# Adjacency products with residual and layer norm: first x in two halves on SyncE's queue, later x on ScalarE's queue, a new order at both ends

## Chip, cores and metric

One core of a Trainium2 chip runs the whole program. The metric is the time of one execution on the device in microseconds (us); less is better.

## What is computed

For each of 8 batches there are x (1024 rows of 128 floats) and an adjacency matrix adj of 1024 x 1024 int32. With these inputs adj holds only 0 and 1, so of the four relations only the first has a mask that is not empty.

```python
masks = (relation[None] == rel_ids[:, None, None, None]).astype(x.dtype)
h = jnp.einsum('rbnm,bmd->rbnd', masks, x)
y = jnp.einsum('rbnd,rdo->bno', h, weight)
...
x = _layernorm(x + y + bias)
```

## The kernel before, in words

A batch is cut into 8 units of 128 rows of adj. The kernel is written engine by engine, each with its own program in a fixed order, and semaphores between them; nothing is scheduled by a planner. What the engines do for a batch b:

- SyncE issues the loads of adj in pairs of units (`load_adj`, 1 MB each, 8 KB in one piece for each partition; the ten units of the start are loaded alone with `load_unit`, 512 KB each in pieces of 4 KB) and of x (`load_x`, 512 KB). adj has three slots, so the load for batch b waits until batch b-3 has been transposed and checked in that place. x has a place of its own for every batch. All these loads, and after them all stores, go through SyncE's one DMA queue (q1 in the profile); only the first x and the bias go through ScalarE's queue (q10).
- `step(b)` says how rows lie on partitions: with step J (8) a partition holds eight neighbouring rows of x, which is one piece of 4 KB; with step 2 it holds two neighbours in four places, so x moves in pieces of 1 KB. For adj it decides the stride at which TensorE reads.
- TensorE transposes each unit (`transpose_unit`), VectorE copies the transposed unit out as a mask (`mask_unit`), TensorE multiplies x by it in two parts, `x_hi` and `x_lo`, for a group of units (`products`), ScalarE copies the result (`copy_h`), and TensorE multiplies that by the weights (`project`). Batches 2 to 6 are two groups of 4 units each. TensorE takes turns: a transposed unit of the next group, then a quarter of the products of this one.
- ScalarE makes `x_hi` (`split_hi`) and reads every pair of adj once more to test that it holds only 0 and 1 (`check`); GpSimd makes `x_lo` from `x_hi`, adds the bias, and normalises the rows; VectorE adds y and x (`sum_rows`) and takes the statistics.
- The last batch is cut finer: groups a (4 units), c (2), e (1) and d (1), with the rows of the last two batches shared out among ScalarE, GpSimd and VectorE, and a matmul with `found` that says whether a second pass for other inputs is needed (it is not entered with these inputs).

The products of a batch wait for the whole `x_hi` of that batch, and `x_hi` waits for the landing of the whole x. ScalarE's program for the groups is one loop: `copy_h` of the group before, in the last group of a batch `split_hi` of the next batch, then the checks, and behind the first of them `root`, the square root for the batch before.

Of the kernel before, what the change touches and what calls it, by code (L numbers as in the profile page):

```python
# [5 lines left out]
P = 128  # L6
FP32 = mybir.dt.float32
# [32 lines left out]
def adj_resnorm_kernel(nc, x, adj, weight, bias, out):  # L40
# [14 lines left out]
    def step(b):  # L55
        return J if b < EARLY else 2
# [61 lines left out]
    with ctx:  # L118
# [9 lines left out]
        ident = sb("ident", [P, P], BF16)  # L128
        ones = sb("ones", [P, 1], FP32)
# [55 lines left out]
        s_unit = [[sem(f"unit_loaded{b}{u}") if alone(b, u) else None for u in range(J)] for b in range(EARLY)]  # L185
        s_x = [sem(f"x_loaded{b}") for b in range(B)]
# [5 lines left out]
        s_ident = sem("ident_ready")  # L192
        s_const = sem("constants_ready")
# [197 lines left out]
        def _(sp):  # L391
            def load_x(b):
                sp.dma_start(units_of(x_sb[:, b], b, 0, J), rows_of(x, b, 0, J)).then_inc(s_x[b], 16)  # L393

# [15 lines left out]
            load_unit(0, 0)  # L410
            load_unit(0, 1)
# [4 lines left out]
            load_x(1)  # L416
# [21 lines left out]
        def _(pool):  # L438
# [3 lines left out]
                                    base=0, pattern=[[-1, P]], channel_multiplier=1).then_inc(s_ident, 1)  # L442

# [58 lines left out]
            normalise(full, full.units[:4])  # L502
# [6 lines left out]
        def _(act):  # L509
            def check(b, k):  # L510
# [15 lines left out]
            def split_hi(b, js, signal):  # L526
                act.wait_ge(s_x[b], 16)
# [24 lines left out]
            split_hi(0, slice(0, HALF), s_hi0)  # L552
            split_hi(0, slice(HALF, J), s_hi)
# [23 lines left out]
            normalise(full, full.units[4:5])  # L577
            copy_h(e)
            root(ra)
            normalise(full, full.units[5:7])  # L580
            copy_h(d)
            normalise(full, full.units[7:]).then_inc(s_aside, 1)
# [286 lines left out]
```

## Time and profile before

| what | value |
|---|---|
| median of 3 runs | 120.64 us (120.59 to 120.68) |
| the profiled execution, whole | 120.54 us |
| its span, first to last instruction | 118.8 us |
| TensorE busy | 106.6 us, 90% |
| ScalarE busy | 88.1 us, 74% |
| VectorE busy | 84.8 us, 71% |
| GpSimd busy | 70.3 us, 59% |
| DMA | 42.22 MB, 355 GB/s over the span |
| granted TensorE clock, mean | 0.985 |

The shares are means over the whole span. The profile further cuts the span in 40 slices, follows the chain of work that ended last, and lists what every engine waited for; times in those views count from the first instruction.

### The profile page before, as it was taken

To read this page: it belongs to the slowest core of one execution; us is meant where nothing else is said; L and a number is where in the kernel's file an instruction comes from. 1 tells how busy PE (TensorE), PEld (TensorE's weight loads), DVE (VectorE), ACT (ScalarE), POOL (GpSimd) and SP (SyncE) were. 2 spreads that over 40 slices of the span, in tenths; PEclk is the share of its full clock that TensorE was granted. 3 is DMA by queue.
4 is the path that set the end of the run, shared out by engine and by line. 5 is a ranking of instruction groups with operands and counts; after the bars stand their busy time and mean duration, and the time that the engine had idled before them with its cause. 6 is when DMAs were issued, how large, how long until landed. Compare 5 with 4: busy or idle time off the path is not lost.

```text
span 118.8 us, 2879 instructions
## 1 busy us (share of the span) xinstructions
PE 106.6 (90%) x1012; PEld 80.4 (68%) x1023; DVE 84.8 (71%) x252; ACT 88.1 (74%) x114; POOL 70.3 (59%) x132
## 2 busy tenths in 40 slices
PE   6788999899999979999999999999999999999400
PEld 2168898799997646767676767676868676679300
DVE  1055678397877848696959887787779777998840
ACT  4088277947797999799999499968987698925530
POOL 2007001940047998399569955995689577977740
PEclk9999999999999999999999999999999999999985
DMA  3999999999999999999999999999999999450271
GB/s 73 389 408 411 414 407 422 414 391 412 425 414 384 419 403 436 380 414 414 419 391 404 422 406 394 420 406 423 377 433 411 415 399 383 141 177 0 85 248 35
DMA packets 12419, 42.22 MB, mean 355 GB/s; under 512 B 882, under 2 KB 7155, under 8 KB 8947
## 3 DMA queue, kind: packets, MB, share of 16 engines
q1 hardware_dynamic: 12256, 41.49, 88.6%
q10 hardware_dynamic: 146, 0.52, 1.3%
q8 instruction: 9, 0.15, 0.5%
q14 instruction: 8, 0.06, 0.1%
HBM read 37.81 MB, written 4.19 MB: 354 GB/s over the span
## 4 chain that ended last, share of the span: by engine, by line
PE 58%; DMA 29%; SPq 5%; DVE 2%; issue 1%; ACT 0%; DVEq 0%
PE h_ps L619 32%; DMA adj_sb<-adj 29%; PE ids_t L601 16%; PE y_ps L633 9%; SPq L396 4%; PE ids_t L633 1%; DVE x_sb L758 0%; SPq L393 0%; SPq L412 0%; ACT std L539 0%; DVE stats L711 0%; DVE x_sb L705 0%; DVE moments L717 0%; DVEq L255 0%; DVE shift L751 0%
## 5 line engine op out<-in xcount | busy, mean ns | idle before, releaser
L522 ACT ACTIVATE junk<-adj_sb,minus 128x2048 bf16<-128x2048 int32 x32 | 63.8, 1994 | 0.4 <-DMA adj_sb<-adj 0.4
L699 DVE TENSOR_SCALAR mask_t<-ids_t 128x1024 bf16<-128x1024 uint16 x64 | 43.6, 687 | 25.2 <-PE ids_t L601 24.1
L601 PEld LDWEIGHTS ids_t<-ident,adj_sb 128*128 128x128 bf16 x512 | 36.5, 123 | 13.8 <-DMA adj_sb<-adj 2.7
L601 PE MATMUL ids_t<-ident,adj_sb 128*128 128x128 bf16 x512 | 40.0, 221 | 2.3 <-DMA adj_sb<-adj 2.2
L619 PE MATMUL h_ps<-mask_t,x_lo 128*128 128x512 bf16 (+2 forms) x184 | 33.5, 314 | 0.0
L619 PE MATMUL h_ps<-mask_t,x_hi 128*128 128x512 bf16 (+2 forms) x173 | 31.1, 310 | 1.2 <-DVE mask_t L699 0.6
L448 POOL TENSOR_TENSOR x_lo<-x_sb,x_hi 128x1024 f16<-128x1024 f32 x7 | 15.0, 2144 | 24.2 <-ACT x_hi L531 24.2
L488 POOL TENSOR_SCALAR x_sb<-x_sb,rstd,shift 128x128 f32<-128x128 f32 x55 | 24.0, 457 | 1.0
L535 ACT ACTIVATE h_all<-h_ps 128x512 f32<-128x512 f32 (+2 forms) x23 | 10.6, 463 | 18.1 <-PE h_ps L619 18.1
L454 POOL TENSOR_TENSOR x_sb<-x_sb,bias_sb 128x1024 f32<-128x1024 f32 x8 | 19.0, 2377 | 7.8 <-DVE x_lo L764 7.7
L619 PEld LDWEIGHTS h_ps<-mask_t,x_hi 128*128 128x128 f16 x184 | 15.6, 98 | 7.2 <-DVE mask_t L699 1.2
L619 PEld LDWEIGHTS h_ps<-mask_t,x_lo 128*128 128x128 f16 x184 | 16.4, 98 | 5.9
L633 PE MATMUL y_ps<-w_sb,h_all 128*128 128x128 f32 x120 | 17.8, 284 | 0.0
L633 PEld LDWEIGHTS y_ps<-w_sb,h_all 128*128 128x128 f32 x120 | 15.0, 192 | 0.1
L711 DVE BATCH_NORM_STATS2 stats<-x_sb 128x6 f32<-128x128 f32 x64 | 14.5, 280 | 0.1
L705 DVE TENSOR_TENSOR x_sb<-y_ps,x_sb 128x512 f32<-128x512 f32 (+2 forms) x20 | 11.0, 552 | 1.9 <-PE y_ps L633 1.0
L531 ACT ACTIVATE x_hi<-x_sb 128x1024 f16<-128x1024 f32 (+1 forms) x9 | 8.5, 954 | 3.1 <-DMA x_sb<-x 3.1
L692 DVE TENSOR_REDUCE row_max<-x_hi 128x8 f32<-128x1024 f16 x8 | 9.6, 1202 | 0.0
L522 ACT ACTIVATION_READ_ACCUMULATOR junk<-adj_sb,minus 128x1 f32 x32 | 6.1, 190 | 0.0
L640 PE MATMUL h_ps<-mask_t 128*128 128x512 bf16 x11 | 4.6, 586 | 1.2 <-DVE mask_t L787 1.2
L717 DVE BATCH_NORM_AGGREGATE moments<-stats 128x2 f32<-128x6 f32 x64 | 5.3, 154 | 0.1
L470 POOL TENSOR_TENSOR product<-sixteenth,first_guess 128x8 f32<-128x8 f32 (+1 forms) x8 | 1.6, 203 | 6.2 <-DVE first_guess L727 6.0
(44 smaller groups left out, 30.8 us busy)
## 6 DMA issues: line engine op xcount, KB each, us to landing
adj_sb<-adj SPq DMA_DIRECT2D x27, 1024.0 KB, 19.5
adj_sb<-adj SPq DMA_DIRECT2D x10, 512.0 KB, 8.4
x_sb<-x SPq DMA_DIRECT2D x7, 512.0 KB, 18.9
out<-x_sb SPq DMA_DIRECT2D x7, 512.0 KB, 16.7
x_sb<-x ACTq DMA_DIRECT2D x1, 512.0 KB, 5.4
out<-x_sb SPq DMA_DIRECT2D x2, 256.0 KB, 3.3
w_sb<-weight SPq DMA_DIRECT2D x1, 64.0 KB, 6.1
bias_row<-bias ACTq DMA_DIRECT2D x1, 0.5 KB
```

The source lines that it names most:

```text
L448: nc.gpsimd.tensor_tensor(x_lo[:, b % 2], x_sb[:, b], x_hi[:, b % 2], ALU.subtract).then_inc(s_lo, 1)
L454: nc.gpsimd.tensor_tensor(x_sb[:, b], x_sb[:, b], bias_sb[:, :].unsqueeze(1).to_broadcast([P, J, D]), ALU.add).then_inc(s_xb, 1)
L488: last = nc.gpsimd.tensor_scalar(rows[:, slot, u, :], rows[:, slot, u, :], rstd[:, slot, u:u + 1], shift[:, slot, u:u + 1], ALU.mult, ALU.add)
L522: nc.scalar.activation(junk[:, at % 2], adj_sb[:, slot, 2 * k:2 * k + 2, :], ACT.Square, scale=2.0, bias=minus[:, 0:1], accum_out=squares[ ...
L535: nc.scalar.activation(h_all[:, g.bank, 0:g.count * P], h_ps[g.bank][:, 0:g.count * P], ACT.Copy).then_inc(s_h, 1)
L601: last = nc.tensor.transpose(bank[:, j, :], words[:, j // step(b), j % step(b), 0, :], ident[:, :])
L619: last = nc.tensor.matmul(h_ps[g.bank][:, 0:g.count * P], part[:, g.b % 2, j, :], mask_t[:, g.b % 2, j, g.cols], start=(j == 0 and part is ...
L633: last = nc.tensor.matmul(y_of(g)[:, n, :], h_all[:, g.bank, n * P:(n + 1) * P], w_sb[:, 0, :], start=True, stop=True)
L692: nc.vector.tensor_reduce(row_max[:, b, :], x_hi[:, b % 2], AX.X, ALU.max, apply_absolute_value=True).then_inc(s_rm, 1)
L699: nc.vector.tensor_scalar(mask_t[:, b % 2, :, u * P:(u + 1) * P], ids_t[u % T_BANKS][:, :, :].bitcast(UINT16), 1.0, None, ALU.mult).then_i ...
L705: nc.vector.tensor_tensor(rows[:, g.b, g.us, :], y_of(g)[:, 0:g.count, :], x_sb[:, g.b, g.us, :], ALU.add).then_inc(s_sum, 1)
L711: last = nc.vector.bn_stats(stats[:, u, :], rows[:, g.b, u, :])
```

## The change

There are four parts.

1. The first x no longer comes by ScalarE's queue. It comes as two halves on SyncE's queue, behind the first unit of adj and ahead of the second, with a semaphore for each half.
2. x of the batches 1 to 7 leaves SyncE's queue. ScalarE issues it on its own queue: in the first group of batch b (in the second for batch 0) the x of batch b+1. `split_hi` moves behind the first check of its group and behind `root`. Batch 1 now has step 2 instead of J.
3. At the start TensorE makes one idle matmul less, and transposes the units 2 and 3 of the first batch a step earlier.
4. At the end TensorE adds the x of the last unit with a matmul by an fp32 identity (`add_x`; GpSimd makes that identity at the start), so VectorE takes statistics of group d from PSUM without `sum_rows`; the matmul with `found` comes behind that; of batch 6's rows ScalarE normalises six instead of four, GpSimd two instead of four.

```diff
     def step(b):
-        return J if b < EARLY else 2
+        return J if b == 0 else 2
...
             load_unit(0, 0)
+            for n in range(2):
+                sp.dma_start(x_sb[:, 0, n * HALF:(n + 1) * HALF, :], rows_of(x, 0, n * HALF, HALF)).then_inc(s_x0[n], 16)
             load_unit(0, 1)
...
             load_unit(1, 0)
-            load_x(1)
             load_unit(1, 1)
             for k in range(1, PAIRS):
                 load_adj(1, k)
-            load_x(2)
-            for b in range(EARLY, B):
+            for b in range(2, B):
                 for k in range(PAIRS):
                     load_adj(b, k)
-                if b + 1 < B:
-                    load_x(b + 1)
...
-            normalise(full, full.units[:4])
+            normalise(full, full.units[:2])
...
+            def load_x(b):
+                act.dma_start(units_of(x_sb[:, b], b, 0, J), rows_of(x, b, 0, J)).then_inc(s_x[b], 16)
...
-            act.dma_start(units_of(x_sb[:, 0], 0, 0, J), rows_of(x, 0, 0, J)).then_inc(s_x[0], 16)
...
                 copy_h(groups[g.index - 1])
-                if ends_batch(g):
-                    split_hi(b + 1, slice(0, J), s_hi)
+                if b + 1 < B and g.place == (0 if b else 1):
+                    load_x(b + 1)
                 todo = range(pairs_checked_by(groups[g.index - 1]), pairs_checked_by(g))
                 for n, at in enumerate(todo):
                     check(at // PAIRS, at % PAIRS)
-                    q = groups[g.index - 2] if g.index >= 2 else None
-                    if n == 0 and q and ends_batch(q):
-                        root(sets[q.b])
+                    if n == 0:
+                        q = groups[g.index - 2] if g.index >= 2 else None
+                        if q and ends_batch(q):
+                            root(sets[q.b])
+                        if ends_batch(g):
+                            split_hi(b + 1, slice(0, J), s_x[b + 1], s_hi)
...
+            def add_x(g):
+
+                pe.wait_ge(s_whole, 1)
+                pe.wait_ge(s_xb, g.b + 1)
+                nc.tensor.matmul(y_of(g)[:, 0, :], whole_ident[:, :], x_sb[:, g.b, g.first, :], start=True, stop=False)
...
             project(e)
+            add_x(d)
+            project(d)
             pe.wait_ge(s_found, 1)
             nc.tensor.matmul(ids_t[0][0:1, 0, 0:2].bitcast(FP32), found[:, :], ones[:, :],
                              start=True, stop=True).then_inc(s_count, 1)
-            project(d)
...
-            for g in (e, d):
-                sum_rows(g)
-                statistics(g)
+            sum_rows(e)
+            statistics(e)
+            statistics_of_sum(d)
```

Three places show how the rows move. On ScalarE, over one batch in the middle (batch 4: the second `x_hi` row is the x of batch 5), the order before is this; L522 is a check, L535 `copy_h`, L531 `split_hi`, L539 `root`.

```order
L535 ACTIVATE h_all<-h_ps 128x512
L522 ACTIVATE junk,squares<-adj_sb,minus 128x2048 x2
L535 ACTIVATE h_all<-h_ps 128x512
L531 ACTIVATE x_hi<-x_sb 128x1024
L522 ACTIVATE junk,squares<-adj_sb,minus 128x2048
L539 ACTIVATE std<-moments,eps 128x8
L522 ACTIVATE junk,squares<-adj_sb,minus 128x2048
```

The same batch in the changed kernel, where L526 is a check, L539 `copy_h`, L535 `split_hi`, L543 `root` and L512 the new load:

```order
L539 ACTIVATE h_all<-h_ps 128x512
L512 DMA x_sb<-x 128x4x256
L526 ACTIVATE junk,squares<-adj_sb,minus 128x2048 x2
L539 ACTIVATE h_all<-h_ps 128x512
L526 ACTIVATE junk,squares<-adj_sb,minus 128x2048
L543 ACTIVATE std<-moments,eps 128x8
L535 ACTIVATE x_hi<-x_sb 128x1024
L526 ACTIVATE junk,squares<-adj_sb,minus 128x2048
```

The load of x stands behind the first `copy_h` of the batch, and `x_hi` one check and `root` later than before; between load and use stand two checks, a `copy_h`, a third check and `root`.

On SyncE, from the start of the program, the rows that go and come (with their - and +) are these; L393 and L412 of the new file are the block's head and the halves of x.

```order
-L396 DMA adj_sb<-adj 128x1024 x2
-L412 DMA w_sb<-weight 128x128
-L396 DMA adj_sb<-adj 128x1024 x7
-L393 DMA x_sb<-x 128x1024
+L412 DMA x_sb<-x 128x512 x2
+L396 DMA adj_sb<-adj 128x1024
+L414 DMA w_sb<-weight 128x128
+L396 DMA adj_sb<-adj 128x1024 x8
+L403 DMA adj_sb<-adj 128x2048 x27
```

Behind the start, SyncE's queue now holds the 27 pairs of adj in one run, with no x between them, and then the stores.

On TensorE, the end before (L619 `products`, L633 `project`, L678 the matmul with `found`):

```order
L619 MATMUL h_ps<-mask_t,x_lo 128x128 x8
L633 MATMUL ids_t<-w_sb,h_all 128x128
L678 MATMUL ids_t<-ones,found 1x1
L633 MATMUL ids_t<-w_sb,h_all 128x128
L255 TENSOR_LOAD again
```

and now, with L647 as `add_x`:

```order
L639 MATMUL ids_t<-w_sb,h_all 128x128
L647 MATMUL ids_t<-x_sb,whole_ident 128x128
L639 MATMUL ids_t<-w_sb,h_all 128x128
L692 MATMUL ids_t<-ones,found 1x1
L258 TENSOR_LOAD again
```

The identity matmul stands between the last two projections, and the matmul with `found` behind both.

## Rows read from the trace of the kernel before

**Rows 1.** Page: span, ScalarE's busy time, and DMA in 40 slices (busy tenths).

```profile
span 118.8 us, 2879 instructions
...
PE 106.6 (90%) x1012; PEld 80.4 (68%) x1023; DVE 84.8 (71%) x252; ACT 88.1 (74%) x114; POOL 70.3 (59%) x132
...
DMA  3999999999999999999999999999999999450271
```

**Rows 2.** Chain that ended last: start us, us, what; its first line gives shares.

```profile
PE 58%; DMA 29%; SPq 5%; DVE 2%; issue 1%; ACT 0%; DVEq 0%
...
24.82 18.44 DMA adj_sb<-adj
...
50.18 0.81 PE h_ps L619 x3
...
62.56 0.81 PE h_ps L619 x3
...
74.93 0.81 PE h_ps L619 x3
...
87.30 0.81 PE h_ps L619 x3
...
99.68 0.81 PE h_ps L619 x3
```

**Rows 3.** Timeline of TensorE around 43 us: start us, us, what, idle before.

```profile
43.30 0.64 PE L601 MATMUL ids_t<-ident,adj_sb 128*128 128x128 bf16 x8 [0.58 <-DMA adj_sb<-adj]
```

**Rows 4.** DMA issues: KB each, median us from issue to landing.

```profile
adj_sb<-adj SPq DMA_DIRECT2D x27, 1024.0 KB, 19.5
...
x_sb<-x SPq DMA_DIRECT2D x7, 512.0 KB, 18.9
...
x_sb<-x ACTq DMA_DIRECT2D x1, 512.0 KB, 5.4
```

**Rows 5.** DMA queues in 2.5 to 4.5 us: packets, MB, share of 16 engines.

```profile
q1 hardware_dynamic: 77, 0.32, 46.6%
q10 hardware_dynamic: 77, 0.32, 38.6%
```

**Rows 6.** DMA packets and q1 in 56 to 60 us.

```profile
DMA packets 252, 1.68 MB, mean 420 GB/s; under 512 B 26, under 2 KB 50, under 8 KB 50
...
q1 hardware_dynamic: 252, 1.68, 101.5%
```

**Rows 7.** DMA packets and q1 in 61 to 63 us, while an x passes.

```profile
DMA packets 341, 0.82 MB, mean 410 GB/s; under 512 B 16, under 2 KB 273, under 8 KB 273
...
q1 hardware_dynamic: 341, 0.82, 109.5%
```

**Rows 8.** Instructions of lines 393 and 403: ns min/median/max, first and last start us.

```profile
L393 SPq DMA_DIRECT2D x_sb<-x x7: 429/1862/3792, 6.3 to 67.8; - x7
...
L403 SPq DMA_DIRECT2D adj_sb<-adj x27: 385/2102/6860, 7.2 to 77.8; - x27
```

**Rows 9.** Timeline of ScalarE: start us, us, what.

```profile
36.89 0.39 ACT L535 ACTIVATE h_all<-h_ps 128x256 f32<-128x256 f32 x1 [0.72 <-PE h_ps L619]
...
49.72 0.60 ACT L535 ACTIVATE h_all<-h_ps 128x512 f32<-128x512 f32 x1 [0.86 <-PE h_ps L619]
50.22 2.00 ACT L522 ACTIVATE junk<-adj_sb,minus 128x2048 bf16<-128x2048 int32 x1
...
52.20 2.00 ACT L522 ACTIVATE junk<-adj_sb,minus 128x2048 bf16<-128x2048 int32 x1
...
56.66 1.05 ACT L531 ACTIVATE x_hi<-x_sb 128x1024 f16<-128x1024 f32 x1
57.61 1.99 ACT L522 ACTIVATE junk<-adj_sb,minus 128x2048 bf16<-128x2048 int32 x1
```

**Rows 10.** ScalarE's groups in 49.7 to 99 us: busy us, mean ns, idle before.

```profile
L535 ACT ACTIVATE h_all<-h_ps 128x512 f32<-128x512 f32 x8 | 4.8, 595 | 6.9 <-PE h_ps L619 6.9
```

**Rows 11.** Timeline of the end: two rows on ScalarE, TensorE's last projection, VectorE's sum and statistics.

```profile
109.50 0.86 ACT L545 ACTIVATE x_sb<-x_sb,shift,rstd 128x128 f32<-128x128 f32 x2
...
110.74 0.49 PE L633 MATMUL ids_t<-w_sb,h_all 128*128 128x128 f32 x2
...
111.26 0.29 DVE L705 TENSOR_TENSOR x_sb<-ids_t,x_sb 128x128 f32<-128x128 f32 x1
...
111.59 0.29 DVE L711 BATCH_NORM_STATS2 stats<-x_sb 128x6 f32<-128x128 f32 x1
```

**Rows 12.** GB/s in 40 slices of 110 to 118.8 us (0.22 us each).

```profile
GB/s 0 0 0 0 0 0 0 37 0 158 340 321 344 340 372 349 145 51 0 0 261 358 303 289 326 400 354 56 14 9 23 33 19 23 23 5 0 0 0 0
```

More of the change, by code:

```diff
@@ L185, in adj_resnorm_kernel @@
         s_unit = [[sem(f"unit_loaded{b}{u}") if alone(b, u) else None for u in range(J)] for b in range(EARLY)]
+        s_x0 = [sem(f"half_of_first_x_loaded{n}") for n in range(2)]
         s_x = [sem(f"x_loaded{b}") for b in range(B)]
@@ L192, in adj_resnorm_kernel @@
         s_ident = sem("ident_ready")
+        s_whole = sem("whole_ident_ready")
         s_const = sem("constants_ready")
@@ L442, in _ @@
                                     base=0, pattern=[[-1, P]], channel_multiplier=1).then_inc(s_ident, 1)
+            pool.wait_ge(s_ident, 1)
+            nc.gpsimd.tensor_copy(whole_ident[:, :], ident[:, :]).then_inc(s_whole, 1)
             def split_lo(b):
@@ L524, in check, with split_hi @@
                                      accum_out=squares[:, at:at + 1]).then_inc(s_check, 1)
-            def split_hi(b, js, signal):
-                act.wait_ge(s_x[b], 16)
+            def split_hi(b, js, loaded, signal):
+                act.wait_ge(loaded, 16)
                 if b >= 2:
@@ L547, in normalise @@
                 return last
-            act.dma_start(units_of(x_sb[:, 0], 0, 0, J), rows_of(x, 0, 0, J)).then_inc(s_x[0], 16)
             act.dma_start(bias_row[:, :], bias.rearrange("(a d) -> a d", a=1)).then_inc(s_bias, 16)
             act.preload_act_table(ACT.Sqrt)
-            split_hi(0, slice(0, HALF), s_hi0)
-            split_hi(0, slice(HALF, J), s_hi)
+            split_hi(0, slice(0, HALF), s_x0[0], s_hi0)
+            split_hi(0, slice(HALF, J), s_x0[1], s_hi)
             act.wait_ge(s_spread, 1)
@@ L576, in _ @@
             copy_h(c)
-            normalise(full, full.units[4:5])
+            normalise(full, full.units[2:3])
             copy_h(e)
             root(ra)
-            normalise(full, full.units[5:7])
+            normalise(full, full.units[3:5])
             copy_h(d)
-            normalise(full, full.units[7:]).then_inc(s_aside, 1)
+            normalise(full, full.units[5:]).then_inc(s_aside, 1)
             root(rb)
@@ L633, in project @@
                     last = nc.tensor.matmul(y_of(g)[:, n, :], h_all[:, g.bank, n * P:(n + 1) * P], w_sb[:, 0, :],
-                                            start=True, stop=True)
+                                            start=g.index < len(groups) - 1, stop=True)
                 last.then_inc(s_y, 1)
+            def add_x(g):
+                pe.wait_ge(s_whole, 1)
+                pe.wait_ge(s_xb, g.b + 1)
+                nc.tensor.matmul(y_of(g)[:, 0, :], whole_ident[:, :], x_sb[:, g.b, g.first, :], start=True, stop=False)
             def idle_turns(n):
@@ L642, in _ @@
             pe.wait_ge(s_still, 1)
-            idle_turns(9)
+            idle_turns(8)
             pe.wait_ge(s_ident, 1)
@@ L654, in _ @@
             products(g, 1, 2)
+            transpose_unit(0, 2)
             g = groups[1]
             products(g, 0, 2)
-            transpose_unit(0, 2)
+            transpose_unit(0, 3)
             project(groups[0])
             products(g, 1, 2)
-            transpose_unit(0, 3)
             for g in groups[2:LAST + 1]:
@@ L712, in statistics, with statistics_of_sum @@
                 last.then_inc(s_st, 1)
+            def statistics_of_sum(g):
+                dve.wait_ge(s_y, g.index + 1)
+                nc.vector.bn_stats(stats[:, g.first, :], y_of(g)[:, 0, :]).then_inc(s_st, 1)
             def combine(r, g, units):
@@ L752, in shift_rows, with normalise @@
                                                in1=rstd[:, r.b, r.us], op0=ALU.mult, op1=ALU.mult).then_inc(s_rstd_last, 1)
-            def normalise(r, units):
+            def normalise(r, u, source):
                 wait_for_rstd(dve, r)
-                slot = r.b
-                for u in units:
-                    last = nc.vector.tensor_scalar(rows[:, slot, u, :], rows[:, slot, u, :], mean[:, slot, u:u + 1],
-                                                   rstd[:, slot, u:u + 1], ALU.subtract, ALU.mult)
-                last.then_inc(s_done, 1)
+                return nc.vector.tensor_scalar(rows[:, r.b, u, :], source, mean[:, r.b, u:u + 1], rstd[:, r.b, u:u + 1],
+                                               ALU.subtract, ALU.mult)
             def split_lo(b, js, hi, lo):
@@ L849, in _ @@
                 part(rb)
-            normalise(rb, rb.units[2:])
+            normalise(rb, e.first, rows[:, rb.b, e.first, :])
+            normalise(rb, d.first, y_of(d)[:, 0, :]).then_inc(s_done, 1)
             second_pass(dve, second_dve)
```

3 lines of the change are left out of this document (1 added, 2 removed).

## The prediction

> **What bounds the kernel now.** I read the page first: DMA stands at 9 tenths in every slice from the second to the 34th, and TensorE is busy 90% of the span [rows 1]. So two resources are nearly full at once, and the chain must say which one ends last where. It gives TensorE 58% and DMA 29% [rows 2]. Its last DMA piece runs from 24.82 us for 18.44 us; there TensorE waits 0.58 us for the first pair of batch 3 [rows 3]. Up to 43.3 us the arrival of bytes sets the pace. From there no DMA stands in the chain, only TensorE: the products of the batches 3 to 7 begin at 50.18, 62.56, 74.93, 87.30 and 99.68 [rows 2] (the units of each are transposed one group ahead). A batch takes 12.37 us, and its products begin only when its whole `x_hi` is there. That is the deadline the change touches.
>
> x meets it now with ease: it rides in SyncE's queue, 18.9 us from issue to landing, but issued far ahead [rows 4, 8]; ScalarE makes the `x_hi` of batch 4 at 56.66, some 5 us ahead of 62.56 [rows 9].
>
> **Part 2, the later x.** Bytes do not change, only their queue. What matters is how the 16 DMA engines share themselves between two queues that are both full. The one place where the trace shows it is the start, when the first x (q10) meets the units of adj (q1), both in pieces of 4 KB: in 2.5 to 4.5 us each queue moved 77 packets [rows 5]. One for one. That fits a turn for each piece, and it fits equally a turn for each so many bytes, since the pieces were of one size. Now they are not: x comes in pieces of 1 KB, and what it meets are pairs of adj in pieces of 8 KB. One for one in pieces gives x one ninth of the bytes.
>
> The durations: in 56 to 60 us q1 moved 252 packets at a share of 1.015 of 16 engines, that is 65 us of engine time; 50 of them were small, about 2 us, so an 8 KB piece takes 63/202 = 0.31 us [rows 6]. In 61 to 63 us, with 341 packets of which 68 were large (21.3 us of 35.0), the 257 pieces of 1 KB took 0.053 us each [rows 7]. x is 512 pieces, 32 for each engine, so its transfer is 32 x (0.31 + 0.053) = 11.6 us. Each adj load gives an engine 8 pieces and one small completion write, which I count as a turn as well: some 3.6 of the 32 turns cost nothing, 1.1 us less, 10.5 us. Around that lies the fixed part: the first x landed after 5.4 us [rows 4] while its 4 KB pieces, 8 for each engine, at an even share of about 0.16 us each would take 2.6 us and the cold start more; I take 1.5 us of the rest. Landing time L = 12.0 us. The bounds are 5.4 us from the nearest row, if 1 KB pieces are served by bytes, and 13 us with all turns paid.
>
> What ScalarE does in that time [rows 9]: `copy_h` 0.50 us from start to start, a check 1.98, `x_hi` 0.95, `root` 0.2. Issue costs 0.43 us, the least that SyncE shows for an x [rows 8]. After the issue come two checks (4.4 us with the issue), then `copy_h`, which waits for TensorE until about 6.2 us after the issue, a check and `root`: ScalarE comes to `split_hi` 8.9 us after the issue. With L = 12.0 it waits 3.1 us. Behind that wait stand a check, `copy_h` of the batch's last group, and then the issue of the next x. So the issues form a ring that TensorE does not set: L + 0.95 + 1.98 + 0.50, with a few hundredths for semaphores L + 3.45 = 15.45 us, against 12.37 us of TensorE. The ring decides from L = 8.9 us on.
>
> Now step by step. The issue of batch 3's x comes behind the `copy_h` at 36.89, at 37.3 us [rows 9]. `x_hi` is ready at issue + L + 1.05.
> - Batch 3: 37.3 + 13.05 = 50.35, needed at 50.18: 0.2 us late.
> - Batch 4: issued 52.75, ready 65.8, needed 62.56: 3.2 late.
> - Batch 5: issued 68.2, ready 81.25, needed 74.93: 6.3 late.
> - Batch 6: issued 83.65, ready 96.7, needed 87.30: 9.4 late.
> - Batch 7: issued at 99.1. The last pair of adj is issued at 77.8 and needs 19.5 us [rows 4, 8], so q1 has run out at 97 us; this x lands in some 4 us, ScalarE's own 8.9 us decide again, and `x_hi` is ready at 109.1, just when TensorE has done batch 6 (99.68 + 9.4). No further loss.
>
> That adj keeps q1 full until then in spite of the late TensorE is an assumption: the last loads, for batch 7, wait until ScalarE has checked batch 4, which it does with the two checks behind the issue at 68.2, by 73 us; the last of them is issued at 77.8 us now. It holds with 5 us to spare.
>
> Batches 1 and 2: x 1 meets adj pieces of 4 KB (0.16 us each, half of 0.31) and lands after 1.5 + 32 x 0.21 = 8.3 us, under the 8.9; x 2 lands after 12 us, and its batch has three checks behind the issue (L522 x3 in the first group), which brings ScalarE to `split_hi` 2 us later than 8.9. I cost both at 0; if that cover is gone, TensorE's wait for adj at 43.30 [rows 3] takes up the first 0.58 us of it.
>
> `x_hi` one check later, 2.2 us: covered by the 5 us above. If x comes in time this costs nothing, for GpSimd's `x_lo` is needed only in the second half of the products. ScalarE's idle time, 6.9 us in four batches or 1.7 for each [rows 10], covers the issue.
>
> **Part 1 and 3, the start.** The first unit of adj no longer shares its way with x, so the first transposes start sooner. But the second unit has the same bytes ahead of it as before, and by 43.3 us the pace is that of bytes: the gain is used up there. 0; the bounds are 0.6 us less, if x 3 is still under way when the first pair of batch 3 lands and so lets it pass (TensorE waited 0.58 us for it), and 0.2 us more, for x 1 in 1 KB pieces instead of 4 KB (512 x 0.053 against 128 x 0.16 us over 16 engines, 0.4 us at most).
>
> **Part 4, the end.** Without `sum_rows` of d, VectorE takes statistics at about 111.35 instead of 111.59 [rows 11]: the last projection at 110.74 now starts behind the identity matmul. That is 0.2 us less on the chain. But ScalarE has two rows more of batch 6 in front of its store, 0.86 us by the two it does at 109.50 [rows 11], and the three last stores move closer together. The stores run at 300 to 370 GB/s with a pause of 0.6 us between them [rows 12]; a later first store fills that pause. I take 0 for the end, between 0.2 less and 0.3 more.
>
> **Sum.** 120.54 for the profiled execution + 9.4 + 0 + 0 = 129.9 us; the median of the runs lies 0.1 above it, so 130.0. In L it goes as 4L - 38.5: 5.5 us at L = 11, and beyond 12.5 it stops growing near 11, since x 6 then finds q1 empty.
>
> **Rivals.**
> - *Bytes, not pieces* (not slower). If the engines share by bytes, or take 4 KB of a queue at a time, x needs 8 x (0.31 + 0.21) = 4.2 us and lands after 5.7: ahead of ScalarE's 8.9. For it: equal packets in rows 5 were equal bytes too. Against it: nothing in these rows packs small pieces together; each 1 KB is a packet of its own in the profile's count [rows 7]. The time is 120.5, from 119.9 (x 3 lets adj pass, and 0.2 at the end) to 120.9.
> - *A whole load in one turn* (not slower). An engine would finish all 9 pieces of an adj load, 2.6 us, and then all of x, 1.7 us; x lands within 6 us, and the time is again 120.5. Against it: in rows 5 both queues moved evenly, where x, which started first, should have been done before q1 moved. The Trainium skill, DMA: Bandwidth & Descriptors, Queues, rings and completion order, says that an engine goes round its queues by whole packets, typically of 9 to 17 descriptors; by that the change would cost nothing, and the even counts do not look like it.
> - *The issue blocks ScalarE* (slower, by another cause). SyncE's issues of x take 1.86 us in the middle and up to 3.79 where its queue is full [rows 8]. If ScalarE's issue is held up behind SyncE's, 1.7 us of idle time [rows 10] cover the median. At 3.8 us the other 2.1 go into each of four batches: 8 us, 129. For it: nothing; the ScalarE queue holds one x only. It decides from about 2.1 us.
>
> **Chances.** Pieces, slow x: 0.60, with 126 to 132.5 as its own range. Bytes or whole loads: 0.35, of which faster 0.22 and the same 0.13. Blocked issue: 0.05. A change of less than 0.2% (0.24 us) can't be told from none here. Slower 0.65, same 0.13, faster 0.22. The likeliest is 130.0; the range must take in the second case, 120.0, and ends at 132.5.
>
> **What would show it.** In the profile after, x on ScalarE's queue lands 11 to 13 us after its issue; ScalarE waits for x at `x_hi` in the batches 4 to 6, about 3 us each; TensorE waits for `x_hi` at the first products of the batches 4, 5 and 6, and its issues lie 15 to 16 us apart. In the short windows behind an issue, packets of q10 and q1 are even in number and one to eight in bytes. I am wrong if x lands in 6 us or so: then ScalarE never waits for x, and the time stays near 120.5. If instead the issue on ScalarE takes 2 us and more, it is the third rival.

## The result

The changed kernel takes 137.26 us (median of 4 runs, 135.47 to 139.75) against 120.66 for the kernel before on the same chip: the ratio is 1.130, with an interval of 1.120 to 1.140. Two of the four runs (137.65 and 139.75) fell in a slower state of the chip, and the ratios, here and below, compare only runs outside it. The forecast was 130.0 us, with 120.0 to 132.5 as its range. The direction and the kind of wait were right, and the time lies outside the range.

The page of the profiled execution (136.88 us, span 135.1) in the lines that answer to [rows 1]. PEclk is the granted clock in tenths; the group lines give busy time and mean length, and behind the second bar the idle time before them and what ended it.

```profile
span 135.1 us, 2882 instructions
...
PE   6769988999937999289996999259999999999700
...
PEclk9999999999996899968999999977999999999975
DMA  4999999999999999999999999999961340004063
...
q1 hardware_dynamic: 9616, 38.34, 71.9%
q10 hardware_dynamic: 3698, 3.67, 7.9%
...
PE 45%; DMA 19%; issue 10%; SPq 7%; POOL 7%; DVE 5%; ACT 2%; DVEq 0%; ACTq 0%
...
L535 ACT ACTIVATE x_hi<-x_sb 128x1024 f16<-128x1024 f32 (+1 forms) x9 | 8.6, 958 | 21.1 <-DMA x_sb<-x 21.0
...
x_sb<-x ACTq DMA_DIRECT2D x7, 512.0 KB, 15.0
```

TensorE's row shows four dips that were not there before, and ScalarE waits 21.0 us in all for x at `x_hi`: 17.6 of them for the x of the batches 2 to 5, the rest for the first x, for which the kernel before waited 3.1 us as well. One x needs 15.0 us from issue to landing as a median. The DMA engines move the same bytes as before and stay full to the 29th slice; what is late is one load among them, not the bytes as a whole.

ScalarE's timeline shows the wait and what stands behind it (start, length, engine, line, operation, idle time before it; ACTq is the queue on which ScalarE issues):

```profile
40.03 1.06 ACT L535 ACTIVATE x_hi<-x_sb 128x1024 f16<-128x1024 f32 x1 [4.09 <-DMA x_sb<-x]
40.04 0.38 ACTq L512 DMA_DIRECT2D x_sb<-x  x1
40.99 0.36 ACT L539 ACTIVATE h_all<-h_ps 128x256 f32<-128x256 f32 x1
41.26 1.99 ACT L526 ACTIVATE junk<-adj_sb,minus 128x2048 bf16<-128x2048 int32 x1
...
48.35 0.60 ACT L539 ACTIVATE h_all<-h_ps 128x512 f32<-128x512 f32 x1 [1.03 <-PE h_ps L625]
48.84 2.00 ACT L526 ACTIVATE junk<-adj_sb,minus 128x2048 bf16<-128x2048 int32 x1
...
56.47 1.06 ACT L535 ACTIVATE x_hi<-x_sb 128x1024 f16<-128x1024 f32 x1 [4.79 <-DMA x_sb<-x]
56.62 0.37 ACTq L512 DMA_DIRECT2D x_sb<-x  x1
```

The x of batch 3 is issued at 40.04 and its `x_hi` starts at 56.47, 16.4 us later. Then the issue of the next x follows within 0.15 us, although `copy_h` (L539) of the group before stands ahead of it in the program: the issue goes out as soon as the wait in front of it is over, not when the queued activations have run. So the loads form a ring, wait for x, issue of the next x, wait for that one, and it is as long as one landing: the issues of x 3 to 6 lie at 40.04, 56.62, 71.80 and 87.96.

TensorE pays. These are the first products of the batches 2, 3, 4 and 5, with TensorE's idle time before them:

```profile
41.40 0.98 PE L625 MATMUL h_ps<-mask_t,x_hi 128*128 128x512 bf16 x2 [2.86 <-issue]
...
57.84 0.59 PE L625 MATMUL h_ps<-mask_t,x_hi 128*128 128x512 bf16 x2 [2.90 <-issue]
...
73.03 0.59 PE L625 MATMUL h_ps<-mask_t,x_hi 128*128 128x512 bf16 x2 [1.21 <-DVE mask_t L712]
...
89.19 0.98 PE L625 MATMUL h_ps<-mask_t,x_hi 128*128 128x512 bf16 x2 [3.85 <-issue]
```

The profile names another releaser or none, but each of the four begins 0.31 or 0.32 us behind the end of its `x_hi` (for batch 3, 56.47 + 1.06 = 57.53, and 57.84): it is `x_hi` that they wait for. The batches 3, 4 and 5 begin at 57.84, 73.03 and 89.19 where [rows 2] had 50.18, 62.56 and 74.93: 7.7, 10.5 and 14.3 us late. Batch 2 begins at 41.40, where the trace of before has 37.48: 3.9 us late. Batches 6 and 7 begin at 103.23 and 115.61 in this trace, both 15.9 us late. The last projection begins at 127.37, where [rows 11] had 110.74: 0.7 more, of which 0.3 comes back behind it, so that the span is 16.3 us longer.

The step from batch 5 to batch 6 holds no wait for x: x 6 was there (its `x_hi` ran at 99.88, ahead of 103.23). It took 14.04 us against 12.37 before, and the windows of this kernel say why. Their columns are the stretch, its length, then for each engine busy time and instructions, the granted clock, the DMA share and GB/s:

```profile
72.00:75.00 3.00, 1.98 (x16) 1.30 (x18) 3.00 (x7) 3.00 (x4) 2.14 (x1) 1.00 1.03 426
75.00:88.00 13.00, 10.29 (x96) 7.42 (x95) 8.38 (x27) 7.12 (x10) 7.29 (x16) 1.00 1.02 408
88.00:91.00 3.00, 1.81 (x9) 1.12 (x11) 1.22 (x1) 3.00 (x4) 2.05 (x1) 0.71 1.00 410
91.00:103.00 12.00, 11.95 (x104) 8.25 (x103) 7.56 (x22) 10.22 (x13) 9.37 (x18) 0.93 0.79 294
```

After the idle time of 3.85 us the granted clock was 0.71 in 88 to 91 us, so part of it at the lower level, 1.2 GHz. The first half of batch 5 then took 7.86 us (89.19 to 97.05), the second, at full clock, 6.18 (97.05 to 103.23): 1.7 us. The clock fell in the same way behind the idle times of 2.86 and 2.90 us (0.68 in 40 to 44 and 0.69 in 57 to 61), and not behind 1.21 us (1.00 in 72 to 75). It costs time only once: in the batches 2 to 4 x came later than TensorE at either clock.

### The profile page after: what moved, and what is told of

Read it like the earlier page. It is cut to its first block, busy times and chain, and to the rows that moved or that the text cites. A ratio compares the mean times of both kernels' runs of the same rounds, so it can differ in the third digit from the quotient of the medians.

```text
span 135.1 us, 2882 instructions
## 1 busy us (share of the span) xinstructions
PE 111.4 (82%) x1013; PEld 82.5 (61%) x1024; DVE 86.3 (64%) x251; ACT 89.1 (66%) x116; POOL 69.6 (52%) x131
## 4 chain that ended last, share of the span: by engine, by line
PE 45%; DMA 19%; issue 10%; SPq 7%; POOL 7%; DVE 5%; ACT 2%; DVEq 0%; ACTq 0%
PE h_ps L625 25%; DMA adj_sb<-adj 19%; PE ids_t L607 14%; PE y_ps L639 6%; SPq L396 4%; SPq L403 3%; POOL x_sb L488 3%; DVE mask_t L712 2%; POOL x_sb L454 2%; ACT x_sb L549 1%; ACT x_hi L535 1%; DVE moments L735 1%; DVE stats L724 1%; SPq L412 1%; POOL x_lo L448 1%
## 5 line engine op out<-in xcount | busy, mean ns | idle before, releaser
L526 ACT ACTIVATE junk<-adj_sb,minus 128x2048 bf16<-128x2048 int32 x32 | 63.8, 1993 | 1.6 <-DMA adj_sb<-adj 1.5
L607 PEld LDWEIGHTS ids_t<-ident,adj_sb 128*128 128x128 bf16 x512 | 37.4, 121 | 16.9 <-DMA adj_sb<-adj 4.6
L607 PE MATMUL ids_t<-ident,adj_sb 128*128 128x128 bf16 x512 | 41.6, 226 | 3.4 <-DMA adj_sb<-adj 3.3
L625 PE MATMUL h_ps<-mask_t,x_hi 128*128 128x512 bf16 (+2 forms) x173 | 34.8, 333 | 11.5 <-issue 9.6
L625 PEld LDWEIGHTS h_ps<-mask_t,x_hi 128*128 128x128 f16 x184 | 16.2, 101 | 18.6 <-issue 11.5
L488 POOL TENSOR_SCALAR x_sb<-x_sb,rstd,shift 128x128 f32<-128x128 f32 x53 | 23.0, 449 | 1.3 <-DVE shift L769 0.4
L535 ACT ACTIVATE x_hi<-x_sb 128x1024 f16<-128x1024 f32 (+1 forms) x9 | 8.6, 958 | 21.1 <-DMA x_sb<-x 21.0
L625 PEld LDWEIGHTS h_ps<-mask_t,x_lo 128*128 128x128 f16 x184 | 16.5, 99 | 6.0
L539 ACT ACTIVATE h_all<-h_ps 128x512 f32<-128x512 f32 (+2 forms) x23 | 10.5, 455 | 13.5 <-PE h_ps L625 13.5
L526 ACT ACTIVATION_READ_ACCUMULATOR junk<-adj_sb,minus 128x1 f32 x32 | 6.0, 188 | 0.0
L549 ACT ACTIVATE x_sb<-x_sb,shift,rstd 128x128 f32<-128x128 f32 x9 | 4.0, 486 | 1.4 <-POOL shift L481 1.1
L652 PE MATMUL h_ps<-mask_t 128*128 128x512 bf16 x10 | 3.8, 539 | 1.2 <-DVE mask_t L802 1.2
```

Source lines behind the costliest of these rows:

```text
L488: last = nc.gpsimd.tensor_scalar(rows[:, slot, u, :], rows[:, slot, u, :], rstd[:, slot, u:u + 1], shift[:, slot, u:u + 1], ALU.mult, ALU.add)
L526: nc.scalar.activation(junk[:, at % 2], adj_sb[:, slot, 2 * k:2 * k + 2, :], ACT.Square, scale=2.0, bias=minus[:, 0:1], accum_out=squares[ ...
L535: nc.scalar.activation(x_hi[:, b % 2, js], x_sb[:, b, js], ACT.Copy).then_inc(signal, 1)
L539: nc.scalar.activation(h_all[:, g.bank, 0:g.count * P], h_ps[g.bank][:, 0:g.count * P], ACT.Copy).then_inc(s_h, 1)
L607: last = nc.tensor.transpose(bank[:, j, :], words[:, j // step(b), j % step(b), 0, :], ident[:, :])
L625: last = nc.tensor.matmul(h_ps[g.bank][:, 0:g.count * P], part[:, g.b % 2, j, :], mask_t[:, g.b % 2, j, g.cols], start=(j == 0 and part is ...
```

## How the two queues share the DMA engines

In 44 to 50 us, with both queues full (columns: packets, MB, share of 16 engines):

```profile
q1 hardware_dynamic: 288, 2.11, 86.2%
q10 hardware_dynamic: 290, 0.30, 14.4%
```

288 and 290: as many pieces of the one queue as of the other, 2.11 MB to 0.30. That is the sharing that the prediction worked with; of its rivals, shares by bytes fell here. The transfer ran from 43.67 to 55.64, 12 us, and the rival of whole loads in one turn fell with it.

Even counts over 6 us would also come out if each queue had turns of nine pieces, and so would a time near 12 us: the 32 pieces of x on an engine would then pass in four turns, each behind an adj load's eight pieces of 0.31 us (an estimate: 4 x 2.5 + 32 x 0.053 = 11.7 us). The first 0.36 us of the transfer (43.64 to 44) tell the two apart:

```profile
q1 hardware_dynamic: 18, 0.13, 88.4%
q10 hardware_dynamic: 17, 0.02, 13.8%
```

The first 17 pieces of x, about one for each of the 16 engines, all start before 43.94, and none starts from there to 44.03. There the second round begins, 0.32 us behind the end of the first piece of x, and a piece of adj takes 0.31 to 0.32. So one piece passes in a turn. The Trainium skill, DMA: Bandwidth & Descriptors, Queues, rings and completion order, has an engine take a whole packet, typically of 9 to 17 descriptors, from one queue before it switches. The measurement decides against it.

What the prediction had not seen is the time ahead of the first piece. The same view for 40.04 to 43.64, from the issue of x 3 until its first piece, has no row for q10 at all:

```profile
DMA packets 212, 1.52 MB, mean 421 GB/s; under 512 B 27, under 2 KB 27, under 8 KB 27
q1 hardware_dynamic: 212, 1.52, 101.5%
issues: line engine op xcount, KB each, median us to landing
adj_sb<-adj SPq DMA_DIRECT2D x1, 1024.0 KB, 21.7
x_sb<-x ACTq DMA_DIRECT2D x1, 512.0 KB, 16.4
```

3.6 us pass, in which SyncE's queue moves 1.52 MB, although every other turn should belong to x. It is the same for each x from 1 to 6: 3.5 to 3.7 us. With SyncE's queue empty (x 7, issued at 102.78) the first piece moves after 1.0 us, and x lands 3.6 us after its issue. So the landing of x 3 is 3.6 us to the first piece, 12 us of transfer and about 0.8 to the semaphore: 16.4. For x 2 to 5 it is 15.0 to 16.5 us, with transfers of 10.6 to 12.3.

## The experiments

### The queue alone, and everything but the queue

`queue_alone` is the kernel before with one part of the change: x 1 to 7 on ScalarE's queue, one batch ahead.

```diff
# ScalarE
                 copy_h(groups[g.index - 1])
+                if b + 1 < B and g.place == (0 if b else 1):
+                    load_x(b + 1)
                 if ends_batch(g):
                     split_hi(b + 1, slice(0, J), s_hi)
# SyncE: load_x(1), load_x(2) and load_x(b + 1) taken out
```

> The kernel before with only the loads of x 1 to 7 moved to ScalarE's queue, one batch ahead; x_hi stays ahead of the check, both ends stay as before. Theory (the queue costs everything): x lands 15 to 16.5 us after its issue and the time is 133 to 140 us. Rival (the other parts share the blame): under 130 us.

137.54 us, ratio 1.136 (1.129 to 1.144). Its ScalarE rows read like those of the changed kernel; the three x waited for are those of the batches 2 to 4:

```profile
39.22 1.06 ACT L527 ACTIVATE x_hi<-x_sb 128x1024 f16<-128x1024 f32 x1 [5.66 <-DMA x_sb<-x]
39.37 0.38 ACTq L504 DMA_DIRECT2D x_sb<-x  x1
...
55.61 1.06 ACT L527 ACTIVATE x_hi<-x_sb 128x1024 f16<-128x1024 f32 x1 [6.62 <-DMA x_sb<-x]
56.21 0.37 ACTq L504 DMA_DIRECT2D x_sb<-x  x1
...
72.51 1.06 ACT L527 ACTIVATE x_hi<-x_sb 128x1024 f16<-128x1024 f32 x1 [4.76 <-DMA x_sb<-x]
```

`x_on_sync` is the changed kernel with the loads of x 1 to 7 back in their old places on SyncE.

> The changed kernel with only the loads of x 1 to 7 put back into SyncE's queue, in their old places. Theory (the queue costs everything): TensorE waits for x_hi nowhere after batch 2, and the time is 120.2 to 121.0 us. Rival (a good part of the 16 us comes from the later place of x_hi, the step of batch 1, or the two ends): above 122 us, with TensorE waiting for x_hi or x_lo although x has landed long before.

122.37 us, ratio 1.011 (1.010 to 1.013), and no wait for a later x is left. So the queue alone makes the whole loss, behind which the other parts don't show; by themselves those cost 1.4 us together, which prediction and expectation had at nothing; they are taken apart below.

### Is it lateness, or the queue as such?

`two_ahead` leaves x on ScalarE's queue and issues it one batch sooner.

```diff
-                if b + 1 < B and g.place == (0 if b else 1):
-                    load_x(b + 1)
+                if b == 0 and g.place in (1, 3):
+                    load_x(1 if g.place == 1 else 2)
+                if b and b + 2 < B and g.place == 0:
+                    load_x(b + 2)
```

> The changed kernel with x of batch b+2 instead of b+1 issued in the first group of batch b (x 1 and x 2 both in batch 0). Theory (x is late by its slow share alone, nothing else of the queue costs): x still needs 15 to 16.5 us, but has some 21, so ScalarE waits for no x and the time is 120.0 to 121.5 us. Rival (traffic on two queues slows adj, or the issue on ScalarE costs): above 123 us.

122.69 us, ratio 1.016 (1.014 to 1.017). x still lands after 16.0 us as a median, and the waits for it are down to 0.2 us in all. That shows the mechanism: what costs is that one batch is shorter than a landing. The number lies 1.8 us above the kernel before and so outside the expectation; 1.4 of it are the other parts', which `x_on_sync` had shown as well.

### The length of the pieces

`adj_4k` loads the pairs of adj from batch 2 on unit by unit, so that x meets pieces of 4 KB; `x_4k` gives x pieces of 4 KB (step J in every batch) and leaves adj at 8 KB.

```diff
# adj_4k
+                for u in (2 * k, 2 * k + 1):
+                    sp.dma_start(adj_sb[:, slot, u:u + 1, :], rows_of(adj, b, u, 1)).then_inc(s_adj[slot][k], 16)
# x_4k
     def step(b):
-        return J if b == 0 else 2
+        return J
```

> The changed kernel with each pair of adj from batch 2 on loaded by two DMAs in pieces of 4 KB instead of one in pieces of 8 KB; x and its place as in the changed kernel. Theory (one piece of x for each piece of adj): the 32 pieces of an engine take 32 x 0.21 = 6.8 us instead of 11.9. If the 3.6 us ahead of the first piece are a number of adj pieces, they halve too, and x lands in 9.5 us, time 120.5 to 122.5; if they are a fixed time, x lands in 11.3 us, time 121 to 126. Rival (x has a fixed share of the bytes, whatever the pieces): x lands after 15 to 16 us as now, time 134 to 139.

> The changed kernel with step J for every batch, so x moves in pieces of 4 KB (128 instead of 512) and adj in 8 KB as now; TensorE reads adj at a wider stride, 0.07 us more for each unit of batches 1 to 7. Theory (one piece for one piece): x takes 8 x 0.47 = 3.8 us behind the first 3.6 and lands about 8.3 us after its issue; no wait for x, and the time is 123 to 126 us by the stride. Rival (an x on this queue is slow by a share of bytes): x lands in 15 us or more, time above 134.

`adj_4k`: 125.37 us, ratio 1.037 (1.035 to 1.039). `x_4k`: 122.47 us, ratio 1.012 (1.010 to 1.014), no wait for a later x, and a little less than expected. In `adj_4k` `x_hi` still waits for x, 8.7 us in six waits, and the last line gives the landing of the ACTq loads (least, median, greatest):

```profile
  ACT x_hi L539: 8.7, 6
...
DMA to landing us min/median/max: 11.3/11.8/12.2
```

The landings in `x_4k`:

```profile
DMA to landing us min/median/max: 6.9/8.6/9.3
```

The transfer follows the turns. With adj pieces of half the length it took 7.5 us (54.95 to 62.42) in place of 12; with a quarter as many pieces of x 4.7 us (54.67 to 59.38). The time ahead of the first piece did not follow: 3.6 and 3.5 us (51.38 to 54.95, and 51.19 to 54.67), with 1.43 and 1.39 MB of SyncE's queue ahead. It is not a number of adj's pieces (some 180 of 8 KB, some 350 of 4 KB), nor of x's.

### Where do the 3.6 us come from?

`three_in_flight` and `two_in_flight` let SyncE issue a pair of adj only when the pair three, or two, before it has landed.

```diff
             def load_adj(b, k):
                 slot = b % ADJ_SLOTS
+                if b >= 2:
+                    c, m = divmod(PAIRS * b + k - 3, PAIRS)   # - 2 in two_in_flight
+                    sp.wait_ge(s_adj[c % ADJ_SLOTS][m], loads_of(c, m))
```

> The changed kernel, where SyncE issues a pair of adj (from batch 2 on) only when the pair three before it has landed, so its queue holds at most 3 MB and never blocks. It tells apart what the 3.6 us between the issue of x and its first piece are. Theory A (ScalarE's descriptors wait behind SyncE's blocked issue): the first piece moves about 1 us after the issue, x lands in 13 to 14 us, and the time falls to 124 to 131 us. Theory B (each engine has a stock of adj pieces taken in already, some ten, whatever SyncE does): 3.3 to 3.8 us stay, x lands in 15 to 16.5 us, time 133 to 139.

> As the run with three pairs of adj in flight, but two. There the first piece of x moved 1.9 to 3.6 us after its issue, in the changed kernel 3.6, with an idle SyncE queue 1.05. Theory A (the delay is waiting behind what SyncE has issued and the queue has not taken in): 1 to 2 us, x lands in 12.5 to 14 us, time 123 to 131 us. Theory B (a time that any full engine adds): 3 us and more remain, time 131 us or above.

`three_in_flight`: 133.14 us, ratio 1.099 (1.096 to 1.103). The time lies in theory B's range, but neither theory held for the delay: the times to the first piece scatter, 2.7, 3.0, 1.9, 3.6 and 2.5 us for x 2 to 6. The shortest, from the issue at 54.85 to 56.7, had 0.72 MB ahead:

```profile
q1 hardware_dynamic: 93, 0.72, 97.9%
```

`two_in_flight`: 126.42 us as the mean of the two runs behind its ratio of 1.046 (1.043 to 1.050), 128.66 as the median of all five; its trace is of a run of 130.52. The times to the first piece go down to 1.0 us for two of the loads and are 2.2 to 3.6 for the others. No x from 1 to 7 is waited for there; TensorE now waits for adj, by up to 1.28 us at a time, since SyncE issues too late to keep the engines full. So the time ahead depends on what SyncE's queue has issued. Limiting it makes the changed kernel faster, but not as fast as the kernel before.

`adj_1k` and `adj_512b` change the rate: from batch 2 on each pair of adj comes as four loads of 256 columns, or eight of 128.

```diff
+                cuts = 1 if b < 2 else 4                      # 8 in adj_512b
+                for n in range(cuts):
+                    cols = slice(n * N // cuts, (n + 1) * N // cuts)
+                    sp.dma_start(units_of(adj_sb[:, slot], b, 2 * k, 2)[..., cols],
+                                 rows_of(adj, b, 2 * k, 2)[..., cols]).then_inc(s_adj[slot][k], 16)
```

> The changed kernel with every load of adj from batch 2 on cut into four loads of 256 columns each, so that adj moves in pieces of 1 KB like x. Bytes theory (SyncE's queue has a fixed 1.4 to 1.5 MB ahead of a newly issued x, as it had at 8 KB and at 4 KB): pieces of 1 KB took 0.053 us each on 16 engines, about 310 GB/s, so x's first piece moves 4.6 to 4.8 us after the issue. Time theory (a fixed delay of the second queue while the first is full): 3.5 us again. Either way x then has half of all pieces and half of the bytes, 512 x 2 x 0.053 / 16 = 3.4 us of transfer.

> The same with eight loads of 128 columns, pieces of 512 bytes. The rate of such pieces isn't known from a run here and is read from this one. Bytes theory: the delay to x's first piece is 1.45 MB divided by that rate, above 5 us if the rate is below 290 GB/s. Time theory: 3.5 us. A third theory, that loads count and not bytes, would give fewer bytes ahead than 1.4 MB in both of these kernels, since each load is now a quarter or an eighth of a pair.

One run each: 129.71 and 176.16 us, beside 120.57 for the kernel before. For `adj_1k` the packets from an x issue at 54.07 to its first piece:

```profile
DMA packets 1338, 1.31 MB, mean 347 GB/s; under 512 B 79, under 2 KB 1336, under 8 KB 1336
q1 hardware_dynamic: 1336, 1.29, 106.6%
```

3.8 us and 1.29 MB. By loads, a pair and a half would have been 0.4 MB: that theory fell. A fixed time (3.5 to 3.6) misses by 5 to 9%, a fixed stock (1.39 to 1.52 MB, at 347 GB/s 4.0 to 4.4 us) by 5 to 15%, so these two are not told apart. In `adj_512b` the small pieces came at 192 to 198 GB/s, SyncE's loads landed 2.9 us after their issue, and q1 held 70 to 72% of the engines; there the first piece of x moved 1.1 us after its issue (63.27 to 64.3), about as with an empty queue. The delay belongs to engines that are full with a backlog behind them. What holds that backlog is not shown.

### The 1.4 us beside the queue

Three kernels go back from `x_on_sync` part by part, and one puts a single part into the kernel before.

```diff
# first_x_back = x_on_sync and, for the two halves on SyncE:
+            act.dma_start(units_of(x_sb[:, 0], 0, 0, J), rows_of(x, 0, 0, J)).then_inc(s_x[0], 16)
# first_x_and_step_back = that and
-        return J if b == 0 else 2
+        return J if b < EARLY else 2
# hi_first = that and, directly behind copy_h (taken out behind the first check):
+                if ends_batch(g):
+                    split_hi(b + 1, slice(0, J), s_x[b + 1], s_hi)
# late_hi_alone = the kernel before, with split_hi moved behind the first check and root
```

> The kernel with x 1 to 7 back on SyncE's queue (122.4 us) and now also the first x back on ScalarE's queue in one load. Theory (of the 1.5 us by which that kernel is behind the one before, about 0.7 come from the first x on SyncE's queue: adj unit 1 landed at 8.23 us instead of 7.60): 121.5 to 121.9 us. Rival (the loss is at the end or by the late x_hi): stays at 122.3.

> As the run with the first x back, and batch 1 has step J again, so its x moves in 4 KB pieces. Theory (x 1 in 1 KB pieces costs another 0.5 us in the stretch where bytes set the pace): 120.9 to 121.3 us. What is left of the change are the order of transposes, the place of x_hi and the new end, which I expect within 0.3 us of the kernel before. Rival: 121.6 or more, then the new end costs.

> The run with the first x and the step back (121.7 us, 0.57% above the kernel before), with split_hi put ahead of its check again; what is left of the change are the order of the first transposes and the new end. Theory (x_hi behind the check makes GpSimd 1.9 us late in batch 7, so the normalising on ScalarE and with it the last copy_h come late, about 0.7 us): 120.6 to 121.1 us. Rival (the new end itself costs, by the rows moved from GpSimd to ScalarE and the longer TensorE order): stays at 121.5 or above.

> The kernel before with nothing changed but split_hi of x 1 to 7 behind the first check and root. Theory (GpSimd's lateness at the end): 0.5 to 0.9 us slower than before. Rival (a check of 2 us is covered by the 5 us between x_hi and its first products, as I predicted): within 0.2%.

| kernel | us | ratio to before |
|---|---|---|
| `x_on_sync` | 122.37 | 1.011 (1.010 to 1.013) |
| `first_x_back` | 122.56 | 1.014 (1.011 to 1.017) |
| `first_x_and_step_back` | 121.70 | 1.006 (1.004 to 1.008) |
| `hi_first` | 120.89 | 1.000 (0.999 to 1.002) |
| `late_hi_alone` | 122.43 | 1.013 (1.010 to 1.015) |

The two halves of the first x cost nothing, where the expectation had 0.7 us. Step 2 for batch 1, which gives x 1 pieces of 1 KB, costs 0.9: in `first_x_back` the first unit of batch 3 is transposed at 44.44, after a wait of 0.54 for adj, in `first_x_and_step_back` at 43.71, in the kernel before at 43.30 [rows 3]. The late `split_hi` costs the next 0.8 (0.7 by the ratios, since the two ran on different chips). What is left in `hi_first`, the order of the first transposes and the new end, costs and brings nothing.

Where the 0.8 of the late `split_hi` goes is read from the pair that differs in it alone. First GpSimd, ScalarE and TensorE at the end of `first_x_and_step_back`:

```profile
97.85 2.14 POOL L453 TENSOR_TENSOR x_lo<-x_sb,x_hi 128x1024 f16<-128x1024 f32 x1 [2.26 <-ACT x_hi L537]
...
109.77 0.20 POOL L486 TENSOR_TENSOR shift<-minus_mean,rstd 128x8 f32<-128x8 f32 x1
...
110.01 0.49 ACT L551 ACTIVATE x_sb<-x_sb,shift,rstd 128x128 f32<-128x128 f32 x1 [1.10 <-POOL shift L486]
...
111.83 0.49 PE L640 MATMUL ids_t<-w_sb,h_all 128*128 128x128 f32 x2 [0.41 <-ACT h_all L541]
```

and in `hi_first`:

```profile
94.90 2.15 POOL L453 TENSOR_TENSOR x_lo<-x_sb,x_hi 128x1024 f16<-128x1024 f32 x1 [1.35 <-ACT x_hi L537]
...
98.61 0.20 POOL L475 TENSOR_TENSOR product<-sixteenth,first_guess 128x8 f32<-128x8 f32 x1 [0.96 <-DVE first_guess L746]
...
107.51 0.20 POOL L475 TENSOR_TENSOR product<-sixteenth,first_guess 128x8 f32<-128x8 f32 x1 [1.00 <-DVE first_guess L746]
...
108.69 0.20 POOL L486 TENSOR_TENSOR shift<-minus_mean,rstd 128x8 f32<-128x8 f32 x1
...
110.99 0.49 PE L640 MATMUL ids_t<-w_sb,h_all 128*128 128x128 f32 x2
```

`x_lo` of the last batch starts 2.95 us later. GpSimd's two waits for VectorE, 0.96 and 1.00, take up 1.9 of it, and its `shift` for batch 6 comes 1.08 late. ScalarE waits 1.10 for it; behind that wait stands, a few instructions on, the last `copy_h`, and the last projection starts at 111.83 and not at 110.99. TensorE itself was only 0.14 us behind when it began the last products (109.71 and 109.57). The other traces agree: wherever `split_hi` is late and x in time (`x_on_sync`, `first_x_back`, `first_x_and_step_back`, `late_hi_alone`, `two_ahead`), the last projection waits 0.40 to 0.51 us for `copy_h` and begins 2.1 to 2.2 us behind the last products; where it is early (`hi_first`, `two_ahead_mended`, the kernel before), it waits for nothing and begins 1.4 us behind them.

`late_hi_alone` lost 1.5 us, more than its expectation had. Its end reads the same, the last projection at 112.52 after a wait of 0.51 for `copy_h`, against 110.74 [rows 11]: 1.8 late, 0.7 more than the 1.08 by which the last products already were (110.39, and 109.31 in the trace of before). Those 1.08 come from the start. A `copy_h` of batch 0, ahead of every `x_hi` that was moved, ran at 18.42, in the kernel before at 15.69. Over the eight traces named above this `copy_h` runs anywhere from 15.54 to 18.42, in no order that follows the edits, and this trace is of the slowest of the kernel's six runs (122.92). So the start's part is not settled, and only the 0.7 at the end is put down to `split_hi`.

### A version with the sound parts

`two_ahead_mended` keeps ScalarE's queue, two batches ahead, and the new end, with the other parts taken back.

```diff
# the changed kernel, with first_x_and_step_back's edits to x 0 and step(), and
                 copy_h(groups[g.index - 1])
+                if ends_batch(g):
+                    split_hi(b + 1, slice(0, J), s_x[b + 1], s_hi)
+                if b == 0 and g.place in (1, 3):
+                    load_x(1 if g.place == 1 else 2)
+                if b and b + 2 < B and g.place == 0:
+                    load_x(b + 2)
```

> x 1 to 7 on ScalarE's queue two batches ahead (122.7 us with the rest of the change), with the first x on ScalarE's queue, step J for batch 1, and split_hi ahead of the check, as before the change; the new end stays. Theory (nothing of ScalarE's queue costs once x has 21 us): 120.4 to 121.1 us, as the run with split_hi first. Rival (x on a second queue delays adj or ScalarE all the same): 0.4 us or more above that run.

121.39 us, ratio 1.004 (1.002 to 1.006), half a microsecond more than `hi_first`, which differs in having x 1 to 7 on SyncE's queue: the expectation's rival came true. From 20 us on TensorE waits for adj at 23.61 (0.61 us) and at 38.18 (0.45), in `hi_first` only at 43.56 (0.56). That fits x taking turns from adj early on; it was not isolated. No kernel here beats the one before.

## Why the prediction was wrong, step by step

**Right.** Turns go piece for piece. x misses its deadline and TensorE waits at the first products, though in the batches 2 to 5 and not 4 to 6; the issues of x 3 to 6 lie 15.2 to 16.6 us apart (forecast 15 to 16), and batch 7 adds nothing. Issue costs ScalarE 0.37 to 0.41 us, so the third rival fell. The halves of the first x and the new end came out near their zeros (`first_x_back`, `hi_first`).

**The step that failed** is the landing time, L = 12.0 us. Its transfer term, 10.5 us, was fair (10.6 to 12.3 measured for x 2 to 5). Its fixed term, 1.5 us, came from the first x [rows 4], which meets queues that have only just begun. Behind a full queue it is 3.6 us to the first piece and 0.8 at the end: L is 16.4. The upper bound of 13 us had only the transfer in it and took the fixed part as known, so the range ended too low as well.

**What followed from it.** x 2 was put at zero, since ScalarE would come to its `split_hi` 10.9 us after the issue. It came 12.5 us after it, so with L = 12.0 the zero would have held; x 2 landed after 16.5 us (issued at 23.47, `x_hi` at 40.03), ScalarE waited 4.09, and batch 2 began 3.9 us late. That put the issue of x 3 at 40.04, 2.7 us behind the forecast's 37.3, and x 3 took 4.4 us longer than forecast: together with the 0.3 us from `x_hi` to the products these are the 7.5 us by which batch 3 missed. x 1 also landed later than forecast, 12.0 us after its issue against 8.3, but just as ScalarE came to it, and nothing waited: `queue_alone`, where x 1 came in 4 KB pieces and was through by 16.23, lost as much.

**Two costs of zero that weren't.** The move of `split_hi` was called covered by 5 us; that was right for TensorE's products and left out GpSimd, whose `x_lo` moves with it and which has only 1.9 us of slack to the end: 0.8 us between `first_x_and_step_back` and `hi_first`. Step 2 for batch 1 was given 0.2 us at most and costs 0.9. Neither adds to the loss of the changed kernel, where the wait for x covers them, except at the end, where the last projection waits 0.41 us for `copy_h`.

**An error that hid part of this.** The ring was taken as L + 3.45, with a check and `copy_h` between the wait and the next issue. The trace shows L + 0.15. With L = 12 that ring would have been 12.15, shorter than TensorE's 12.37, and the loss small; 15.45 came out near the true 15.2 to 16.6 by two errors against each other. That is luck, and so is the good part of the agreement in the batches 4 and 5 below.

**The sum again.** Forecast against trace, in lateness added: up to batch 3, 0.2 and 7.7 (half of it in batch 2); batch 4, 3.0 and 2.8; batch 5, 3.1 and 3.8; batch 6, 3.1 and 1.7; batch 7, none and none; end, 0 and 0.4. Together 9.4 and 16.3. The 1.7 of batch 6 is the clock, which the forecast did not price: x 6 found q1 running out, landed after 10.2 us and was in time. The missing 7 us are in the start of the ring, before the first batch that the forecast had late by more than 0.2.

One argument about the rivals was too short as well. The prediction says that by turns of whole packets the change would cost nothing; with turns of nine pieces for each queue the transfer would have been as long as measured. Only the order of the first pieces settled it.

The chances were stacked rightly on the slow side (0.65), but the price of this case was known only from the first load of the program, and the range did not say so.

## What to carry to other kernels

In these runs a load's landing time is a time to its first piece, which depends on how far the other queue has been issued ahead, and a transfer, which depends on turns: as many as it has pieces, each as long as one piece of each queue. Before a load moves to a second queue beside a full one, compare that sum with the lead it is issued with; a lead of two batches (`two_ahead`), or pieces of 4 KB for x (`x_4k`), took all but 1.8 and 1.5 of the 16.6 us away here. And when an engine's step is moved within its slack, follow each engine that reads its result to the end of the program: the slack of TensorE was not GpSimd's.

## What was not expected of the hardware

- The first piece of a load on ScalarE's queue moved 3.5 to 3.7 us after its issue while SyncE's queue was full, 1.0 us with that queue empty, and in between (1.0 to 3.6) when SyncE was held to two or three pairs. Pieces of adj of 8, 4 and 1 KB gave 3.6, 3.6 and 3.8 us.
- ScalarE's issue ran ahead of activations that stand before it in its program: 40.04 against 40.99 for the `copy_h` ahead of it.
- adj in pieces of 1 KB moved at 347 GB/s, in pieces of 512 bytes at 192 to 198 with the engines' share at 70 to 72%, against about 410 in pieces of 8 KB (one run each).
- A TensorE idle for 2.86 to 3.85 us came back at the lower clock for a while (a group of products in 7.4 to 7.9 us, not 6.2); after 1.21 us it did not.
